# New step orders for all five engines of a gated cross-attention and expert kernel

## What is computed

```python
Q = (x_text @ Wq).reshape(Bb, Tt, H, DH)            # 4 heads of 32
K = (x_vision @ Wk).reshape(Bb, Gg, H, DH)          # 1024 context rows
scores = jnp.einsum('bthd,bghd->bhtg', Q, K) / np.sqrt(DH)
topv, topi = jax.lax.top_k(scores, K_TOP)           # the 32 largest of 1024
attn = zeros.at[..., topi].set(softmax(topv))
c_t = jnp.einsum('btg,bgd->btd', attn.mean(axis=1), x_vision @ Wv)
x = layernorm(x_text); x = x * (1 + gate * scale_in) + gate * shift_in     # FiLM from c_t
y = s4d(x, ...)                                     # a long convolution, done by DFTs
y = y * (1 + gate * scale_out) + gate * shift_out
xt = x_text + y; xt = xt + gelu(layernorm(xt) @ W1 + b1) @ W2 + b2
out = x + tanh(g) * layernorm(xt)
# then: each token to its best of 8 experts (SwiGLU), plus a shared SwiGLU expert
```

## Time and profile before

| | |
|---|---|
| median of 3 runs | 1616.59 us (1614.28 to 1619.75) |
| profiled execution | 1618.56 us |
| its span, first to last instruction | 1616.8 us |
| granted TensorE clock, mean | 0.974 of full |
| PE busy, share | 1447.7 us, 90% |
| DVE | 1343.2 us, 83% |
| ACT | 1170.1 us, 72% |
| POOL | 1124.9 us, 70% |

### The profile page before, as it was taken

The page is one execution under the profiler, slowest core; times in us unless marked ns, Lnnn a source line. Parts: engine busy times, 40 slices in busy tenths (PEclk is TensorE's granted clock), DMA queues, the critical chain, the costliest instruction groups (busy, mean ns, idle before and its releaser), DMA issues. The chain is left out here.

```text
span 1616.8 us, 22044 instructions
## 1 busy us (share of the span) xinstructions
PE 1447.7 (90%) x7027; PEld 1049.3 (65%) x7035; DVE 1343.2 (83%) x1937; ACT 1170.1 (72%) x2349; POOL 1124.9 (70%) x1275
## 2 busy tenths in 40 slices
PE   6888789899989988998989999999988998989996
PEld 4555556576657665766676757666665775766996
DVE  7999999999999998998988899989988999336221
ACT  2799965987598759876897699768976698143442
POOL 1589957678867886789678977897689866602232
PEclk9889999999999999999999999999999999999998
DMA  8200221012101310124323411342134211665322
GB/s 231 74 4 6 68 64 33 14 33 73 27 13 27 82 23 14 34 72 114 102 71 80 122 56 41 94 109 85 27 95 114 60 33 31 203 216 172 65 47 24
DMA packets 97223, 115.25 MB, mean 71 GB/s; under 512 B 17840, under 2 KB 74168, under 8 KB 96964
## 3 DMA queue, kind: packets, MB, share of 16 engines
q1 hardware_dynamic: 85348, 100.32, 21.4%
q0 software_dynamic: 11760, 13.52, 5.3%
HBM read 75.48 MB, written 19.58 MB: 59 GB/s over the span
## 5 line engine op out<-in xcount | busy, mean ns | idle before, releaser
L1443 DVE MAX8 R<-ZB 128x8 f32<-128x1024 f32 x384 | 468.1, 1224 | 10.0
L1447 DVE MATCH_REPLACE8 ZB<-R,ZB 128x1024 f32<-128x1024 f32 x256 | 309.3, 1208 | 0.0
L1007 ACT ACTIVATE R<-PS 128x512 f32<-128x512 f32 (+6 forms) x404 | 174.7, 464 | 138.0 <-PE PS L2116 36.7
L704 POOL TENSOR_TENSOR ZB<-ZB 128x1024 f32<-128x1024 f32 x95 | 209.0, 2200 | 76.0 <-ACT ZB L1004 72.0
L706 POOL TENSOR_TENSOR ZB<-ZB 128x1024 f32<-128x1024 f32 x95 | 224.1, 2359 | 7.4
L1877 PE MATMUL PS<-R 128*128 128x256 f32 x776 | 208.9, 395 | 12.9 <-ACT R L1007 9.4
L1436 DVE MAX8 R<-PS 128x8 f32<-128x1024 f32 x128 | 156.7, 1224 | 40.9 <-PE PS L1900 40.1
L1877 PEld LDWEIGHTS PS<-R 128*128 128x128 f32 x776 | 144.7, 197 | 48.8 <-ACT R L1007 13.7
L1039 ACT ACTIVATE ZB<-PS,R 128x1024 bf16<-128x1024 f32 x128 | 141.5, 1105 | 42.4 <-POOL ZB L704 27.8
L1439 DVE MATCH_REPLACE8 ZB<-R,PS 128x1024 f32<-128x1024 f32 x128 | 155.3, 1214 | 0.0
L1004 ACT ACTIVATE ZB<-PS,R 128x1024 f32<-128x1024 f32 x128 | 142.3, 1112 | 3.0
(11 more groups left out here) (282 smaller groups left out, 3097.4 us busy)
## 6 DMA issues: line engine op xcount, KB each, us to landing
ZR<-ZR SPq DMA_DIRECT2D x96, 128.0 KB
ZB<-in_L_ffn_rt_gate SPq DMA_DIRECT2D x21, 512.0 KB, 4.1
ZB<-in_L_ffn_rt_up SPq DMA_DIRECT2D x21, 512.0 KB, 5.0
ZB<-in_L_ffn_rt_down SPq DMA_DIRECT2D x21, 512.0 KB, 4.6
R<-in_x SPq DMA_DIRECT2D x16, 512.0 KB, 4.0
ZB<-in_ctx SPq DMA_DIRECT2D x8, 768.0 KB, 5.0
R<-xs_d SPq DMA_DIRECT2D x39, 128.5 KB, 2.1
out<-R SPq DMA_DIRECT2D x32, 128.0 KB, 1.9
```

Of the source, the lines that this page charges most:

```text
L704: pool.tensor_tensor(e, e, keep, ALU.mult).then_inc(s.g_att, 1)
L1007: return act.activation(o, i, ACT.Copy, **k)
L1443: vec.max(ml[:, 8 * r:8 * r + 8], w).then_inc(s_tk[n % 2], 1)
L1447: vec.match_replace(w, ml[:, 8 * r:8 * r + 8], w, NEG).then_inc(s_tk[n % 2], 1)
```

## The change

All five order strings are replaced, and PE_WARM with them. Each string has the same characters in the same numbers as before, in another order: 57 of 218 places differ on SP, 191 of 514 on POOL, 944 of 1627 on ACT, 328 of 1114 on DVE, 395 of 889 on PE. Within a part the steps keep their order, so no part's code changes. PE_WARM holds 384 constant products in place of 390. The ACT program gets 119 loads of an activation table in place of 117, since the place of a step decides which table is there when it comes. One wait in DVE's setup step is written as a count of what has been issued instead of the number 2, because that step no longer comes first.

```diff
 POOL_ORDER = (
-    "22733311111410111101010121011131011110011110111010301103002055055505505505505555055305200550005355550530505660"
...
+    "27233311111410111101101101110121011310011131011101001103200055055505555300555555050025550050200535555050350560"
...
 PE_ORDER = (
-    "03533333333554545151544545145656533156563151552255166525516652515556165355231235665125525166133222166213551555"
...
+    "03353333333545551455454145451656335516653515555166225512551665552133561365525215665152551266133222166213551555"
...
 PE_WARM = (
-    "07304541015025000030200010100100143002310022330001210012530001301341010012400000000100530010231300020101533000"
...
+    "04400121231910160032000000000000020311000512323131000120120010326200103000330201300102340100103301120130115001"
...
-                on.wait_ge(own.sem, 2)
+                on.wait_ge(own.sem, own.n)
                 vec.tensor_copy(qt[96:97, :, :], ones[96:97, 0:1].unsqueeze(2).broadcast_to([1, H, 768])).then_inc(s.v_ones, 1)
```

More of the change, by code:

```diff
@@ new lines @@
+    "66650555055555500555555055555005505532000205355550503505660665055505555550055550555505550250355500030555550532"
+    "00656506650705555555550558550058505555500855550032020555553058053556006667055555555580505553085505555058055055"
+    "00202055555305803550650666070855555505550555538055505555282055535000300555550580056650667055508055555550555508"
+    "05555555500585000505555505805606665557555888588566665555999999999999999999")
+ACT_ORDER = (
+    "33344333466645656755010100006553767704010001670701010076316001000460777102010026301020013607376700100201330000"
+    "71163016770000022010006711776000001012200007171647220000001020177001104260000016100660001616882200100012281008"
+    "00041110000400100018880010001888220000018138010000128831030000188880300002018888100200011011020083808010001330"
+    "88388800100248122200000081182884010108089100010098922290000001120800801818288000800811040000114000100222180888"
+    "10800008000018381018280000131880883010001888080010021330002000118880100010833838880010018240022200081180288410"
+    "10800890010901008909020011282000800811228800810080801400000114221000008120811808000800081100238380301880100330"
+    "10008808810888800012208100330011300101000888888802100010482220004081180288001010889920010100088991200200180001"
+    "00022188488000018a088a100400a11a00000a118a200a02000181a00088018800008018a2188a10288180102000200008881881301303"
+    "08010020803001813808a88880203031aa0023102040801281884008a1880100090090011280a922910000021880082880081a18840a00"
+    "00001004101aaa100000118880020200018881aa000018381880200000118888001020018888020100201300130002183301010088808a"
+    "3888200231800023010a00841018a28800480001128890001190a0801900091220a010002882100080018808a8100a00481a1a400a1100"
+    "0820021800008118088010002383382a38830833010300104000881888808100002110020001104880010010a888a88010800aa8220100"
+    "0220811820880101000889910000188099100020a22108000011880020a00211888a000018018aa00a10100002000211a8188008100880"
+    "000080028a88a12188180000188880800221001a001100008010100888822288800a1a008102a000080182a88821801099100000000118"
+    "892292288888888aa8aa88888aa8a888a8aa8a8a8899899b8bbb888bbbbbbbbbbbbbbbbbbbbbbbbbbbbbbbb")
@@ new lines @@
+    "515772221727331777713771777172221771777172777172271771731332331222231777aaa91aaa21aa222a1aaa217777133377772211"
+    "27777771277177177777172271771713332133222213777a9a1aaaa1aa222a1aa217a27771333777172221777771721777177717777223"
+    "7137317712332212321777aaaa2199aaaa122a21aa21a3377b771bb3bb77177bb71b22b7b17777b12b77b217772277177721777171bb23"
+    "3bb232133237717b9a9aaab21aabaa1222aa21aa777b1373bb3771b771bbb7717227717bb1277771772777172271271771bb32223b3133"
+    "b237717929a1aabaaa1aba212b2aa127aa71b7bb733bb31b777721277777712bb127773333371777717722713717b71bb2bb12222177a7"
```

66 lines of the change are left out of this document (21 added, 45 removed).

## The result

| | before | changed |
|---|---|---|
| median, 20 runs each on one chip | 1619.16 us (1614.28 to 1624.53) | 1621.62 us (1618.21 to 1624.40) |
| ratio | | 1.0018, 95% interval 1.0010 to 1.0025 |
| profiled execution | 1618.56 us | 1623.44 us |
| its span | 1616.8 us | 1620.1 us |
| granted clock, mean | 0.974 | 0.970 |

The change costs 2.9 us (0.0018 of 1619; the medians alone differ by 2.5). That is inside the 0.3% that I had called no change, but its interval excludes 1, and it has the other sign than the forecast of 1610.0.

A forecast was written before the change was run, and what follows sets the result against it. DVE was taken to bound the stage from 60 to 1376 us, PE the rest. Terms -5.8 + 0 + 0 + 0.3 - 1.1 = -6.6 took the profiled 1618.6 to 1612.0, the median to 1610.0 us; range 1596 to 1628.

The forecast's parts named there:

- start: Before 60 us: PE's first products start later, DVE's copies end near 16.15 us; +0.3 us, bounds 0 and +1.3.
- score tiles: Between tiles' first MAX8s: 14.8 us less PE surplus over DVE, at ratio 0.39, shortens DVE's waits for products; -5.8 us.
- DVE's other waits: First stage, DFT, router, reciprocal and expert steps: waits of some 38 us exchange evenly; 0, with 8 us to each side.
- remainder: Behind the last tile: the scatter-add moves behind three L869, so DVE's wait for output additions ends earlier; -1.1 us.
- the clock as a rival: Ten more gaps on PE let its clock fall, each costing about 1.2 us, half reaching DVE; 1616 us, chance 0.06.
- slower rival: New tight places: PE's surplus lies elsewhere, at tiles 59, 80, 101, 103, and turns into DVE waits; 1628 us, chance 0.22.
- Nothing to be had: Rival: ACT's and POOL's delays set the waits, so only start and remainder count, -0.8 us; 1616 us, chance 0.22.
- better fit: Rival: the order fits the engines, and DVE's first-stage waits shrink by 25 us; 1591 us, chance 0.10.
- ACT's room and table loads: First stage: room DVE leaves ACT hardly changes, two more table loads fall in ACT's idle time; 0, up to +2.6 us.

The follow-up runs named there:

- e1: Changed kernel with the old orders of all five engines up to about 75 us: 1615.61 us, ratio 0.9980 to the kernel before.
- e3: Kernel before with the new orders of all engines only from about 75 to 1054 us: 1613.02 us, ratio 0.9967 to the kernel before.
- e9: Kernel before with the new orders from about 75 to 1054 us and again from about 1372 us: 1610.94 us, ratio 0.9964.
- e5: Kernel before with the new orders of all engines only up to about 75 us: 1622.95 us, ratio 1.0024.
- e8: Changed kernel with PE's L1989 behind the second half of L2029 again and ACT's copies put back to match: 1620.90 us, ratio 1.0015 to the kernel before.
- e11: Changed kernel with 23 in place of 9 constant products ahead of the first half of L2029: 1617.05 us, ratio 0.9996 to the kernel before.
- e12: Kernel before with the new orders of all engines only from about 1054 to 1372 us: 1628.75 us, ratio 1.0059.
- e13: Kernel before with the new orders only from about 1372 us to the end: 1615.78 us, ratio 0.9985.
- e4: Changed kernel with the old orders from about 1376 us to the end: 1623.87 us, ratio 1.0043 to the kernel before.
- e10: Kernel before with only POOL's scatter-add L968 moved behind the three L869 that follow it: 1619.69 us, ratio 1.0004.
- e2: Changed kernel with the old orders of all five engines from about 1054 to 1124 us: 1621.11 us, ratio 1.0016 to the kernel before.
- e7: Changed kernel with three DVE selection steps of tile 101 moved ahead of the four spectrum steps: 1620.31 us, ratio 1.0014 to the kernel before.
- e6: Changed kernel with POOL's selection pair L704/L706 put back behind two FiLM pairs and the fold L793/L794: 1624.11 us, ratio 1.0037 to the kernel before.
- e18: Changed kernel with both e6's POOL move and e7's DVE move: 1623.83 us, ratio 1.0034 to the kernel before.

## Why the prediction was wrong

Two steps failed. The start was mis-sized, and the term for the score tiles had nothing in it for the order of POOL's work, with DVE's other waits priced at 0. By the lags of the two traces, start, tiles and remainder are +4.3, +2.8 and -3.8 us, where I had forecast +0.3, -5.8 and -1.1. Lags come from one execution each: e1, e3 and e9 have the same orders up to M, and their lags at L are -10.3, -7.7 and -9.3. For the end of the kernel the ratios carry the argument.

- **Start, +0.3 forecast, about +4 measured** (e5 +3.9; e1 gives 6 by difference). I compared DVE's order up to 16 us, found it the same from there, and wrote that the shift "goes through to the first MAX8". The first part was already 1.4 to 1.6 us (15.70 for 14.10), at my upper bound of 1.3 and over it. The first four products took 3.78 us where I had taken 2.7: eight records at 0.47 us each, the pace of the lower clock (4 records in 1.91 us at 41.63 us in the kernel before), and my 0.67 us for a product was a mean over both levels. The larger part, 3.6 us, lies at 41 to 56 us, where DVE's order is indeed the same but PE's isn't: L1989 ahead of the second L2029, and at the lower clock. e8 and e11 each take some 1.8 us off the first MAX8, one by the order, one by the clock. I had the clock as a rival, but looked for it in the gaps between tiles. There it didn't act (0.98 in both kernels).
- **Score tiles, -5.8 forecast for all of them.** Up to 1054 us the new orders gain 5.3 us (e3), so the static surplus of PE over DVE did point the right way for that part. L1436's waits fell by 3.6 us as the term says, and DVE's other waits grew by 6.2, which is inside my 8 us but on the wrong side. From M to E the new orders lose: 9.6 us alone (e12). In combination the end tells less, 2.6 us between e1 and e9 with 3.3 to a side, though the lag grows by 9 in all five traces with these orders there. The working had no term in it for POOL. I had read its share as an average, 70% of the span, and took its order's effect as part of "DVE's other waits, 0". At the place of the loss it is busy at 93 to 95%, and its order changes there.
- **The slower rival** put the loss into L1436's waits, 52.6 us in all, with single ones of 4 us and more at tiles 59, 80, 101 and 103. These waits fell to 36.5 us. At tile 59 the wait is 1.50 us (0.14 before), at 80 1.51 (none), at 101 0.32 (none), at 103 2.65 (2.34). So they did grow at these tiles, by 3.5 us in all, but none came near 4. The neighbourhood of 101 to 103 was right, the wait there was L1643's.
- **Remainder, -1.1 forecast, -2.4 measured** (e13; -4.0 by e4, -0.5 by e9). The sign was right, the size too small. The scatter-add gives 0.6 to 1.0 us in one trace and nothing that the time can show (e10). What makes the rest is open: it lies partly ahead of L1643, where a transfer ends the wait, and partly between L1643 and L1399. The steps that change places on PE here, a FILM_OUT step and DFT steps among them, I had priced at 0; no run moved them, or SP's and ACT's, alone.
- **The other rivals.** "Nothing to be had" falls with e3, where the new tiles alone give 5.3 us. The better fit came nowhere near its 25 us.
- **ACT's room and table loads, 0.** No run speaks against it, none tests it alone.

By the mirror runs, start, early tiles, late tiles and remainder are +3.9, -5.3, +9.6 and -2.4, together +5.8 for +2.9 measured. Along one chain of runs, from the changed kernel over e1, e9 and e3 to the kernel before, the same four are +6, -5.3, +2.6 and -0.5. These must add up to the 2.9, and each has an interval of 2 to 3 us to a side. So what a piece is worth depends on what stands around it. What stays open is why: from N to E the lag of e2 grows by 5.9 us with the new orders behind old ones, that of the changed kernel by 2.6 with new behind new, and no run took those 250 us apart.

## What to carry to other kernels

Sum the work of every engine that an order moves over short stretches, not over a stage: the engine that is at 79% in the mean may be at 95% where the order changes, and there its order has to fit what the others want first. Look at what PE runs right behind a wait: here small matmuls on the path stood there and ran at the lower clock. 14 unread products more, up to the end of the wait, gave back 3.6 us by the ratios; the kernel before had unread products behind its wait and its small matmuls last. When orders of several engines are searched for together, compare them at points where both have issued the same steps, cut there, and keep the better piece: pieces chosen so gave 8.9 us, while the steps moved on one or two engines gained nothing that could be told (e7, e8, e10) or made things worse (e6, e18).

## What the runs showed that I had not expected

- L1989, 32 matmuls of one column, follows the clock as wide products do: 6.83 us at the lower level, 3.63 at the upper, some 213 and 113 ns apiece. Each has a weight load of 128 columns beside it, and these take as long, before and changed:

```profile
46.67 3.76 PEld L1989 LDWEIGHTS PS<-R 128*128 128x128 f32 x32
```

```profile
43.45 7.16 PEld L1989 LDWEIGHTS PS<-R 128*128 128x128 f32 x32
```

- Once down, the clock stayed down: 9 us after the unfilled wait the second L2029 still takes 1.92 us, against 1.06 in e11. In the kernel before it was up again some 5 us after its wait, with constant products in between (10 records in 2.32 us at 44.73 us). More constant products behind the wait, in the new order, weren't tried.
- A lag can vanish and come back. In e5 it is +4.2 us at 52 us, +0.6 at 319 and +5.8 at 1372.
